# A fused attention and expert kernel: output projection rewritten from fp32 to three fp16 products

## What is computed

```
q, k, v = layernorm(x) @ wq.T, wk.T, wv.T        # 16 heads of 64
q, k    = rotary(q), rotary(k)
probs   = softmax(causal(q @ k.T / 8))
a       = concat_heads(probs @ v) @ wo.T         # the output projection: 1024 -> 128
x       = x + layernorm(a)
x       = x + layernorm(ffn(layernorm(x)))       # linear, SwiGLU, 8 experts + shared, linear, SwiGLU
```

## Time and profile before

| | before |
|---|---|
| median of 3 runs | 1312.89 us (1311.67 to 1315.08) |
| the profiled execution's own time | 1314.52 us |
| its span in the profile | 1312.8 us |
| busy: PE, DVE, ACT, POOL | 1152.0, 994.7, 932.3, 956.3 us |
| mean granted clock of PE | 0.956 of full speed |

### The profile page before, as it was taken

One profiled execution on the slowest core, in us unless ns is written; L12 is line 12 of the kernel. 1 busy time (PEld: TensorE's weight loads), 2 busy tenths in 40 slices (PEclk: granted clock), 3 DMA queues, 4 the chain that ended last, 5 costly groups with the idle time before them and its releaser, 6 DMA issues. The chain is left out here.

```text
span 1312.8 us, 34709 instructions
## 1 busy us (share of the span) xinstructions
PE 1152.0 (88%) x13520; PEld 784.5 (60%) x13520; DVE 994.7 (76%) x2153; ACT 932.3 (71%) x2057; POOL 956.3 (73%) x992
## 2 busy tenths in 40 slices
PE   4369999999999999999999899999998398898983
PEld 1126676767766676766666676667776154555551
DVE  7678787878878787878779787877754748787857
ACT  2158878788787878778787878788897665554543
POOL 5439988898887989898888989888675424454524
PEclk8579999999999999999999999999999599999997
DMA  5433515252442515252442515252200400000002
GB/s 178 110 87 76 130 34 130 53 126 73 109 112 52 130 34 131 63 127 66 103 108 55 130 34 130 63 124 72 70 3 2 136 1 1 1 2 0 0 0 64
DMA packets 51147, 95.87 MB, mean 73 GB/s; under 512 B 7088, under 2 KB 23728, under 8 KB 49072
## 3 DMA queue, kind: packets, MB, share of 16 engines
q1 hardware_dynamic: 50992, 93.76, 29.2%
HBM read 56.89 MB, written 33.55 MB: 69 GB/s over the span
## 5 line engine op out<-in xcount | busy, mean ns | idle before, releaser
L652 POOL TENSOR_TENSOR Plo<-P,Phi 128x512 f16<-128x512 f32 (+3 forms) x640 | 537.7, 865 | 139.9 <-ACT P L387 139.3
L384 ACT ACTIVATE Phi<-psS 128x512 f16<-128x512 f32 (+3 forms) x768 | 383.6, 500 | 162.9 <-PE psS L253 114.8
L387 ACT ACTIVATE P<-psS 128x512 f32<-128x512 f32 (+3 forms) x640 | 306.2, 479 | 0.0
L271 PE MATMUL psO<-V,Plo 128*128 128x65 f16 x2304 | 287.8, 194 | 0.0
L267 PE MATMUL psO<-V,Phi 128*128 128x65 f16 x2304 | 287.5, 192 | 0.0
L269 PE MATMUL psO<-V,Phi 128*128 128x64 f16 x2304 | 287.2, 192 | 0.0
L247 PE MATMUL psS<-Q,K 128*128 128x512 f16 (+3 forms) x768 | 251.2, 327 | 38.3 <-DVE Plo L510 32.5
L559 DVE TENSOR_REDUCE pmax<-psX 128x1 f32<-128x512 f32 x384 | 254.3, 682 | 25.8 <-PE psX L328 15.9
L250 PE MATMUL psS<-Q,K 65*128 65x512 f16 (+3 forms) x768 | 251.5, 327 | 0.0
L328 PE MATMUL psX<-K,Q 128*128 128x512 f16 (+3 forms) x768 | 226.5, 330 | 24.2 <-DVE pmax L559 8.5
L267 PEld LDWEIGHTS psO<-V,Phi 128*128 128x128 f16 x2304 | 218.7, 98 | 39.7 <-POOL Plo L652 4.3
(11 more groups left out here) (162 smaller groups left out, 2184.6 us busy)
## 6 DMA issues: line engine op xcount, KB each, us to landing
K<-k_way SPq DMA_DIRECT2D x45, 512.0 KB, 6.9
k_way<-HL SPq DMA_DIRECT2D x60, 256.0 KB, 3.7
q_way<-HL SPq DMA_DIRECT2D x60, 256.0 KB, 4.0
Q<-q_way SPq DMA_DIRECT2D x60, 256.0 KB, 7.1
Q<-q_way SPq DMA_DIRECT2D x15, 512.0 KB, 12.0
x<-in_x SPq DMA_DIRECT2D x4, 512.0 KB, 5.3
out<-x SPq DMA_DIRECT2D x8, 256.0 KB, 2.2
y<-in_x SPq DMA_DIRECT2D x3, 512.0 KB, 10.5
```

The source lines that it names most:

```text
L271: mm = nc.tensor.matmul(O, M.Plo[:, U % NP_, k * P:(k + 1) * P], V[:, HD:2 * HD + 1], start=False, stop=j == t, skip_group_check=True)
L384: nc.scalar.activation(M.Phi[:, U % NP_, 0:w], X, ACT.Exp, scale=SCALE)
L387: nc.scalar.activation(full, X, ACT.Exp, scale=SCALE).then_inc(S.exp_done, 1)
L652: nc.gpsimd.tensor_tensor(M.Plo[:, U % NP_, 0:w], M.P32[:, U % NP_, 0:w], M.Phi[:, U % NP_, 0:w], ALU.subtract).then_inc(S.lo_pool, 1)
```

## The change

The transposed outputs `OT` and the projection weights `wo` are each kept as two fp16 halves, a high half and the remainder. The projection becomes three fp16 products per block (high by high, high by low, low by high). ACT writes the high half of `OT` and signals DVE with a new semaphore; DVE, one step after the item's own (`TURN_LAG = 1`), subtracts the high half from the PSUM bank, writes the low half and gives the bank back. The weights land in the first half of `On` and are split in slot -1 at step 6, by ACT and then by DVE.

```diff
-X_STATS, X_RECIPROCAL, X_NORMAL = 6, 9, 26
+X_STATS, X_RECIPROCAL, X_NORMAL, WO_EARLY = 6, 9, 26, 6
+TURN_LAG = 1
...
+    wo32 = M.On[:, 0:TT // 2, :].rearrange("p a n -> p (a n)").rearrange("p (k d) -> p k d", d=D)
+    turns = sorted((x for x in number if x[1] == "tr"), key=lambda x: number[x])
... PE, item "wo"
-                        pe.wait_ge(S.wo_in, 16)
+                        pe.wait_ge(S.wo_lo, 1)
                     taken(pe, (s - 1, "tr", 0, half))
                     taken(pe, (s, "tr", 1, half))
                     for k in range(4):
+                        t = 4 * half + k
                         for c in range(CH):
-                            t = 4 * half + k
-                            mm = nc.tensor.matmul(X[:, k * P:(k + 1) * P], M.OT[:, c, t * P:(t + 1) * P],
-                                                  M.wo[:, CH * og + c, :], start=c == 0, stop=c == CH - 1)
+                            for i, (oi, wi) in enumerate([(0, 0), (0, 1), (1, 0)]):
+                                mm = nc.tensor.matmul(X[:, k * P:(k + 1) * P], M.OT[:, oi, c, t * P:(t + 1) * P],
+                                                      M.wo[:, wi, CH * og + c, :], start=c == 0 and i == 0,
+                                                      stop=c == CH - 1 and i == 2)
... ACT, item "tr"
-                    nc.scalar.copy(M.OT[:, a[0], a[1] * BANK:(a[1] + 1) * BANK], X).then_inc(free(item), 1)
+                    nc.scalar.copy(M.OT[:, 0, a[0], a[1] * BANK:(a[1] + 1) * BANK], X).then_inc(S.turned_hi, 1)
... ACT, in the loop over steps
+                if s == -1 and u == WO_EARLY:
+                    act.wait_ge(S.wo_in, 16)
+                    nc.scalar.copy(M.wo[:, 0], wo32).then_inc(S.wo_hi, 1)
... DVE
+            def turned_lo(item):
+                s, kind, *a = item
+                if kind != "tr":
+                    return
+                cols = slice(a[1] * BANK, (a[1] + 1) * BANK)
+                dve.wait_ge(S.turned_hi, turns.index(item) + 1)
+                nc.vector.tensor_tensor(M.OT[:, 1, a[0], cols], M.psX[:, bank(item), :], M.OT[:, 0, a[0], cols],
+                                        ALU.subtract).then_inc(free(item), 1)
... DVE, out_scale
+                if n == 0:
+                    dve.wait_ge(S.wo_lo, 1)
... DVE, in the loop over steps, ahead of the step's side items
+                if s == -1 and u == WO_EARLY:
+                    dve.wait_ge(S.wo_hi, 1)
+                    nc.vector.tensor_tensor(M.wo[:, 1], wo32, M.wo[:, 0], ALU.subtract).then_inc(S.wo_lo, 1)
+                for item in at.get((s, u - TURN_LAG), []) if s <= LAST else []:
+                    turned_lo(item)
...
                 for item in at.get((s, u), []) if s > LAST else []:
+                    turned_lo(item)
                     side(item)
... SP
-            sp.dma_start(M.wo[:], I["wo"]).then_inc(S.wo_in, 16)
+            sp.dma_start(wo32, I["wo"]).then_inc(S.wo_in, 16)
... tiles
-        M.wo = sb(stack, "wo", [P, HEADS * HD // P, D], F32)
+        M.wo = sb(stack, "wo", [P, 2, HEADS * HD // P, D], F16)
-        M.OT = sb(stack, "OT", [P, CH, T], F32)
+        M.OT = sb(stack, "OT", [P, 2, CH, T], F16)
```

More of the change, by code:

```diff
@@ L1477, in build @@
         S.wo_in = sem("wo_in")
+        S.wo_hi = sem("wo_hi")
+        S.wo_lo = sem("wo_lo")
+        S.turned_hi = sem("turned_hi")
         S.w_lo_pool = sem("w_lo_pool")
```

## The result

The changed kernel takes 1336.88 us (1335.33 to 1338.08, 4 runs) against 1312.47 us before: a ratio of 1.018, with a 95% interval of 1.016 to 1.020. It is slower by 24 us where 28 were forecast (1341, range 1327 to 1353).

What follows compares the result with a forecast made beforehand. Attention was taken as bound by PE, which works in order and stops for late banks. Slots 1 to 13 +26.1, slot 14 +0.7, slot 0 +0.2, slot 15 -0.5, end -0.4, start +2.2: +28.3, so 1341 us, range 1327 to 1353.

Steps and rivals of the forecast that it cites:

- The products: Projection items on PE: 24 fp16 pairs at 56 ns, 1.34 us for 1.89; of 1.10 us per slot 0.66 arrives.
- The late banks, steps 12 and 16: PE waits for the transposes' bank, given back by DVE's subtraction: 1.31 and 1.19 us per slot in slots 1 to 13.
- Steps 33 and 37: DVE's added operation returns a bank late to the step-36 transpose: 0.17 us per slot, slots 0 to 14.
- The start: Slot -1: DVE's extra split of the weights delays the first scores by 2.2 us, ends 0 and 2.3.
- Slots 1 to 13: Thirteen equal slots, two stalls plus 0.17 us less the products' 0.66 us each: +26.1 us.
- Slot 14: No qk item at step 11, so only the second stall stands: +0.7 us.
- The end: Behind the last slot: two subtractions cost about 0.7 us, the 32 passes save 1.1; together -0.4 us.
- The fp16 pairs run at the pace of their loads: Projection items keep 1.89 us because loads are not hidden, all gain goes: 1352 us; chance 0.07.
- The bank is back in time: Steps 12 and 16: DVE's subtraction ends before PE comes, no stall, full gain: 1298 us; chance 0.07.
- The new stalls replace the old ones: PE's waits of some 2.3 us per slot are DVE backlog that the new pauses clear: 1311 us; chance 0.06.
- A part of the stall is caught up: POOL, ACT or DVE clear some delay in the pause, half the stalls go: 1325 us; chance 0.08.

Runs made afterwards that it cites:

- the fp32 one: Kernel before, fp32 products and copies kept, plus a DVE subtraction one step after each transpose item that only then gives the bank back: 1348.66 us, ratio 1.0272.
- at step 4: Changed kernel with the transposes last in their step and the weights' split at step 4 of slot -1 instead of 6: one execution 1305.51 us, median 1310.58 us.
- the substitute operation: Changed kernel, but ACT gives the bank back and DVE's 64 subtractions read the cosine table in SBUF instead of the bank: 1330.72 us, ratio 1.0146.
- the best one: Changed kernel with transposes last in their step, weights split at step 46, transposes at steps 10 and 14 instead of 11 and 15: 1306.70 us, ratio 0.9958.

## Why the prediction was right, and where it was off

**The account of a regular slot.** From 58.1 us: the products take off 0.62 (57.46), DVE's load adds 0.67 (58.13), and the held bank adds 1.92 (60.05). The products' 0.62 come again with the bank held: 60.67 to 60.05. Together they are 1.97 us, where 2.0 were forecast. Where in the slot they lie can be read from the starts of the transposes in the two profiles:

| from the transpose of step to that of step | before | after | change | forecast |
|---|---|---|---|---|
| 32 to 36 | 4.04 | 4.20 | +0.16 | +0.17 |
| 36 to 11 | 22.92 | 22.98 | +0.06 | 0 |
| 11 to 15 | 5.19 | 6.51 | +1.32 | +1.31 |
| 15 to 32 | 25.94 | 26.37 | +0.43 | 1.19 - 0.66 = +0.53 |

The split into load and hold depends on the order in which they are taken away: without the hold the load costs 0.4 us before the projection (5.1 us in 13 waits), and in the changed kernel no such wait is seen.

**The products.** Right: 56 ns each, an item 1.34 us. Only part of the 1.10 us per slot arrives; I had worked out 0.66 by the `v` item between the projections and DVE's unbroken run behind them, and 0.62 arrives. That it is the `v` item which limits it was not tried.

**The late banks, steps 12 and 16.** Right in mechanism, place and size: 1.31 and 1.19 us forecast, 1.32 and 1.20 read, 27 waits of 27. That it is the held bank is shown by three runs: without the hold but with the load it is gone, with the hold on fp32 products it is there, and with the same subtractions behind a later-wanted bank it is gone.

**Steps 33 and 37.** I charged 0.17 us, and the table above reads 0.16 for the first and 0.06 for what follows the second.

**The start** was mis-sized: "one more operation of 128x1024, 2.28 us, or 2.2 in a row, as the split of `wv`". I took the duration from an operation of the same shape and not from one with the same company. In the kernel after it is

```profile
57.27 1.22 DVE L657 TENSOR_TENSOR wo<-On,wo 128x1024 f16<-128x1024 f32 x1
```

and the first scores come 1.2 us later (93.40 against 92.21), not 2.2. POOL is idle there. The first scores of the other kernels with this split come at 93.64 to 94.14, so the 1.2 is good to some tenths of a us.

**Slots 1 to 13** were forecast 6 us too high: "13 x (1.31 + 1.19 + 0.17 - 0.66) = 26.1" takes 13 equal slots. Regular ones grow by 1.9 to 2.0 us, but the kernel before had slots that weren't regular, and it is these that make up the 6 us. The stretch from step 36 to step 11 of the next slot, 22.92 us where it is regular, is longer in eight cases of 13, by 5.8 us in sum; in the kernel after it takes 22.97 to 23.00 in all 13. Two causes, which cover 5.5 of the 5.8, are read from the traces; neither was tried.

In four of these stretches, those from slots 0, 8, 10 and 12, DVE is held up in the join of the maxima at step 40, which makes them 0.67 us longer each. Its small copy from SBUF to SBUF takes 0.28 us in slot 1 and 1.74 in these four. The timeline of DVE in slots 0 and 1, then of POOL in slot 0, kernel before:

```profile
141.65 1.74 DVE L580 COPY pmax<-pmix 128x8 f32<-128x8 f32 x1
202.33 0.28 DVE L580 COPY pmax<-pmix 128x8 f32<-128x8 f32 x1
```

```profile
139.94 3.42 POOL L652 TENSOR_TENSOR Plo<-P,Phi 128x128 f16<-128x128 f32 x5
```

The row of five POOL operations ends at 143.36 and the copy at 143.39. `low` comes late behind it, and PE waits 1.36 us for it in place of twice 0.30. In the kernel after the copy takes 0.50 to 0.72 us in slots 0 to 13, and PE's wait of 1.36 us is in none. Of the experiments, the fp32 one included, only the one with the subtraction in the transposes' own step has a copy above 0.75 us, once, with 1.54. What moves DVE against POOL there was not tried.

At the start of three slots (5, 10, 11) PE waited for the DMA of the row maxima, 1.02, 0.40 and 0.85 us, and their stretches are 2.8 us longer together; one such row of the kernel before:

```profile
384.26 0.39 PE L247 MATMUL psS<-Q,K 128*128 128x512 f16 x1 [1.02 <-DMA Q<-mrow]
```

In the kernel after such a wait is seen only before the first scores, and slot 5, which had the 1.02, grew by 0.86 alone. The fp32 kernel with the held bank has these waits at the same three slots (1.32, 0.20 and 0.94 us), and no kernel with fp16 products has one at slots 1 to 13. What ties them to the fp32 kernels is open.

**Slot 14** grew by 2.7 in place of 0.7. It holds a wait that I didn't foresee, for the queries' DMA, in the kernel after:

```profile
945.31 0.32 PE L331 MATMUL psX<-K,Q 128*128 128x384 f16 x1 [1.52 <-DMA Q<-q_way]
```

No other trace here has this wait, that of the fp32 kernel with still longer slots included, so longer slots alone don't seem to bring it. Without it the slot would have grown by some 1.2 us.

**The end** was right: -0.2 for -0.4. From the last slot's step-32 transpose to the last projection it takes 0.7 us more, as forecast, since this projection waits 1.1 us for a subtraction; from there to the last write of `y` it takes 1.0 us less.

**Luck.** The total missed by 4 to 5 us and no more because misses of opposite sign met: slots 1 to 13 came out 6 us lower and the start 1 us, slot 14 2 us higher, 1.5 of it by a wait for a DMA, and 0.6 us more came outside attention, which no term had.

**The rivals.** "The fp16 pairs run at the pace of their loads" falls with the 1.34 us. "The bank is back in time" falls with the 27 waits, and its time, 1298, would have been close: without subtractions the kernel takes 1302. "The new stalls replace the old ones" falls: from 150 to 1020 us the wait for `low` is 25.1 us, where it was 29.5, and 3.0 of these 4.4 are the four held-up copies; the wait for the maxima rose from 7.0 to 9.1. "A part of the stall is caught up" has the nearest time (1325) but falls as well: a regular slot grows by 1.97 of the 2.01 us, and only some 0.16 us of the second stall is made good before step 32.

## What to carry to other kernels

Before an operation takes over the freeing of a shared buffer, find the next user of that buffer in the plan and the queue in front of the operation: here 64 subtractions cost some 8 us as work and 27 us as holders of a bank. An order in which the buffer is wanted one or two items later gave the 27 us back. To forecast a sum over slots, look at every slot of the kernel before and not at one: the irregular ones were worth 6 us here. And an engine's busy share (DVE's 76%) says nothing of the moment at which its next operation can start.

## What the runs showed of the hardware

- A DVE subtraction with both inputs in SBUF doesn't run beside a POOL operation that is under way; it seems to start when that one ends. 1024 columns took 1.22 us with POOL idle, 1.82 us at step 4, and 2.28 us in slot -2, where the POOL operation from 26.24 ended at 28.01 and DVE's at 29.09. The last two ended 1.07 and 1.08 us behind POOL. With 512 columns (the substitute operation) it was 0.55 us in 34 of 64 cases. The changed kernel's subtraction from PSUM took 0.68 to 0.69 us in all 64 cases.
- The Trainium skill, SBUF — State Buffer, "SBUF: two separate sides", states this as a rule: a DVE operation with two SBUF inputs and a GpSimd operation that reads SBUF take a shared pair of ports in turn, and the later one is blocked for the whole of the other. The traces here agree, with the ends named above.
- A DVE copy from SBUF to SBUF of 8 columns is held up as well: in slots 0 to 14 of the kernel before it took 0.28 to 1.74 us and ended 0.03 to 0.04 us behind a POOL operation each time.
- A program of one core scatters between executions here, by 2.1 to 7.5 us from lowest to highest in six kernels with 9 to 12 executions (1304.9 to 1312.35 in the best one), so that a single execution can't rank two kernels 1 us apart: the 1305.51 became a median of 1310.58.
